# Waits put at their use, loads in another order, and one-head attentions on products of their weights, in a twelve-stage Perceiver kernel

## The chip, the cores and the metric

The kernel is one program on one core of a Trainium2 chip. The metric is the device time of one execution in microseconds (us). The core has five engines with a queue of instructions each: TensorE (PE), VectorE (DVE), ScalarE (ACT), GpSimd (POOL) and SyncE (SP). SP does nothing here but issue DMAs. The engines meet through semaphores; DMAs run on 16 DMA engines that all queues share.

## The reference

A residual stream `x` of 32 x 32 tokens by 256 features goes through four layers, each a cross-attention to a context of 32 batches x 257 rows x 192 features, a self-attention (or a scan) and a feed-forward part, all in float32, each on the layer norm of `x`:

```python
x = x + _L0_xattn_ref(_layernorm(x), ctx_768, ...)   # 16 heads
x = x + _L0_attn_ref(...)
x = x + _L0_ffn_ref(...)                             # fp4 weights and activations
x = x + _L1_xattn_ref(..., ctx_768, ...)             # 16 heads, clipped
x = x + _L1_attn_ref(...)                            # one head
x = x + _L1_ffn_ref(...)
x = x + _L2_xattn_ref(..., ctx_768, ...)             # 16 heads of 64
x = x + _L2_attn_ref(...)                            # a scan
x = x + _L2_ffn_ref(...)                             # experts with capacity
x = x + _L3_xattn_ref(..., ctx_768, ...)             # one head
x = x + _L3_attn_ref(...)                            # one head, below
x = x + _L3_ffn_ref(...)                             # eight experts
```

The two one-head self-attentions, each over the 32 tokens of a batch:

```python
# L1: f = x Wq^T, g = x Wk^T, h = x Wv^T
scores = einsum('bsd,btd->bst', f, g); beta = softmax(scores, axis=1)
o = gamma[0] * einsum('bsc,bst->btc', h, beta) + x
# L3: q, k, v = x W^T + b
qk = einsum('bsd,btd->bst', q, k)
theta = 0.5 + 0.2 * sigmoid(qk) + 0.15 * tanh(qk) + 0.1 * relu(qk)
out = einsum('bst,btd->bsd', softmax(theta), v) @ Wo.T + bo
```

## The kernel before

The 1024 tokens are `TILES` = 8 tiles of 128, one token to a partition, and `x` stays in SBUF for the whole program; one tile holds 4 batches (`PER_TILE`) of 32 tokens (`SEQ`). `CD` = 2 is the number of 128-row pieces of the 256 features. There are twelve stages one after the other: xattn0, attn0, the fp4 stage, xattn1, attn1, lowrank, xattn2, scan, moecap, xattn3, attn3, moe. A stage is one block with a function for each engine, which writes out by hand the order of that engine's queue: nothing is scheduled by a planner, and an instruction that waits holds everything behind it in its queue. A stage ends in a barrier of all five engines, SP's queue included. Each stage begins with a layer norm (class `Norm`, L95): statistics on DVE, 1/deviation on POOL, then transposes on PE (L190) with some dummy matmuls (L50, `warm` and `keep_busy`) around them.

What the change touches:

- **xattn2** is `stage_wide_attention` with `first=False`. SP's queue (L467 to L545) loads the weights wq and wk, then for the first four batches the two prepared layouts of the context (`load_parts`, L476 and L477), then `last`, wv and wo (L503 to L507), and then the raw rows of the context (`raw_last` L539, `load_rows` L537), of which DVE computes statistics (L888) for a later stage. DVE has those statistics in its queue between the units of the attention. A unit is one of 256 steps (batch and group of heads): scores (PE L668 to L672), their maximum (DVE L860), exp (ACT L785), the scaling (L790), transposes (PE L679), and the product with the context.
- **xattn1** is `stage_clipped_attention`. Its ACT queue waits for all of wv's loads ahead of the first unit of its loop:

```python
            for t in range(ALL + UNITS):
                j, s = divmod(t, UNITS)
                if t == 0:
                    act.wait_ge(wv_loaded, 64)
```

  The bias bv that these loads bring is read in `values` (L1297) alone, which comes first in unit 22. Here POOL scales the probabilities (L1110), DVE clips (L1345) and takes maxima (L1347).
- **attn1 and attn3** are `stage_one_head` (L1703). PE makes q^T and k^T in 8 blocks of two matmuls 128x512 (L1783), and between them v in 8 blocks of two matmuls 128x256 (L1790); then 64 matmuls of 32x32 for the scores, on four column groups of the array (L1799), dummy matmuls while DVE and ACT do the softmax, and then the product with v (L1809). attn1 adds it to x with one DVE instruction per tile (L1891). attn3 (`soft_theta`) scales it (L1901), transposes it (L1816), multiplies by wo (L1825), and adds (L1905). SP in attn3 first loads the stage's own eight tensors and then the expert weights of moe, 16 loads of 1024 KB (`ew.sp`, L2884 and L2885). moe's own small tensors (L2464 to L2467) are loaded in the moe stage; its gate matmuls (L2481) and two POOL instructions (L2472, L2473) wait for them.
- **The fp4 stage**: ACT makes |x| in four pieces (`x_parts`) and then copies the first transposed tile (`turned_x(0)`).
- **xattn3** has a ring of three tiles for the context (`RING`), in two layouts: keys (`load_keys`, L3255 to L3257) and rows (`load_rows`, L3263 and L3264). SP's queue issues both in turn. Keys of tile t may be overwritten when scores(t-3) are done, rows of tile t when the product pv(t-3) (L3363, L3366) is done:

```python
            load_rows(0)
            for t in range(1, TILES):
                load_keys(t)
                load_rows(t)
```

  Ahead of these it loads `last_stat` and `rstd` (L3267, L3269), which DVE and POOL wait for. The short weights of the stage (`ShortWeights`, L3159) are loaded in the scan stage, two stages earlier.

## Time and profile before

| what | value |
|---|---|
| median of 3 runs | 1784.45 us (1783.11 to 1786.04) |
| the profiled execution | 1781.79 us |
| its span in the trace | 1779.9 us, so 1.89 us lie around the span |
| busy shares | PE 89%, DVE 60%, ACT 48%, POOL 43% |
| mean granted clock of PE | 0.963 |
| xattn0, attn0, fp4 start at | 5.1, 351.2, 420.6 us |
| xattn1, attn1, lowrank start at | 519.3, 779.7, 818.9 us |
| xattn2, scan, moecap start at | 835.7, 1187.2, 1317.0 us |
| xattn3, attn3, moe start at | 1437.3, 1524.45, 1574.3 us |

A stage's start is its first layer-norm statistics instruction on DVE. All times in the rows are microseconds from the span's start. A timeline row joins neighbouring instructions of one form ("x8"); a matmul of these float32 tiles is two records, so "x8" is four matmuls. What stands in brackets at a row's end is how long the engine had been idle before it, and what released it. The granted clock is given as a share of the full 2.4 GHz: 1.00 is 2.4, 0.50 is 1.2 GHz.

### The profile page before, as it was taken

To read this page: it belongs to the slowest core of one execution; us is meant where nothing else is said; L and a number is where in the kernel's file an instruction comes from. 1 tells how busy PE (TensorE), PEld (TensorE's weight loads), DVE (VectorE), ACT (ScalarE), POOL (GpSimd) and SP (SyncE) were. 2 spreads that over 40 slices of the span, in tenths; PEclk is the share of its full clock that TensorE was granted. 3 is DMA by queue.
4 is the path that set the end of the run, shared out by engine and by line. 5 is a ranking of instruction groups with operands and counts; after the bars stand their busy time and mean duration, and the time that the engine had idled before them with its cause. 6 is when DMAs were issued, how large, how long until landed. Compare 5 with 4: busy or idle time off the path is not lost. (4 is left out here: it accounts for less than half of the span.)

```text
span 1779.9 us, 37424 instructions
## 1 busy us (share of the span) xinstructions
PE 1592.1 (89%) x13583; PEld 1347.5 (76%) x13583; DVE 1069.7 (60%) x3001; ACT 849.0 (48%) x2446; POOL 771.7 (43%) x924
## 2 busy tenths in 40 slices
PE   7999999888886999987799999989978968859998
PEld 6898998756556999955799988965658934549997
DVE  5888887446855888845676677647971132363332
ACT  5666666355335888842566666641003312213332
POOL 7656656243338999833211111116743411212332
PEclk9999999999998999999999999999988987989999
DMA  8555454110023334302433333325028265771222
GB/s 274 168 174 161 151 174 153 64 63 2 1 83 98 137 130 139 119 19 71 171 122 102 125 104 103 126 79 182 1 54 263 29 179 163 249 243 35 37 38 30
DMA packets 127221, 205.30 MB, mean 115 GB/s; under 512 B 21034, under 2 KB 92362, under 8 KB 126530
## 3 DMA queue, kind: packets, MB, share of 16 engines
q1 hardware_dynamic: 119746, 193.61, 33.4%
q0 software_dynamic: 6720, 8.79, 3.2%
q8 instruction: 111, 1.82, 0.4%
q14 instruction: 68, 0.56, 0.1%
q10 hardware_dynamic: 576, 0.52, 0.1%
HBM read 162.54 MB, written 41.14 MB: 114 GB/s over the span
## 5 line engine op out<-in xcount | busy, mean ns | idle before, releaser
L879 DVE TENSOR_SCALAR xattn_oT<-banks,xattn_last 128x256 f32<-128x256 f32 x256 | 111.7, 478 | 90.8 <-PE banks L699 90.6
L785 ACT ACTIVATE xattn_probs<-banks,xattn_negmax 128x257 f32<-128x257 f32 x256 | 123.6, 483 | 67.5 <-DVE xattn_negmax L860 67.5
L1110 POOL TENSOR_SCALAR xattn_probs<-xattn_probs,xattn_rsum 128x257 f32<-128x257 f32 x128 | 119.6, 935 | 30.0 <-DVE xattn_rsum L1351 29.8
L790 ACT ACTIVATE xattn_probs<-xattn_probs,xattn_rsum 128x257 f32<-128x257 f32 x256 | 131.8, 515 | 1.4 <-DVE xattn_rsum L864 1.4
L860 DVE TENSOR_REDUCE xattn_negmax<-banks 128x1 f32<-128x257 f32 x256 | 106.4, 415 | 34.7 <-PE banks L672 33.3
L679 PE MATMUL banks<-ident,xattn_probs 128*128 128x128 f32 x512 | 104.2, 286 | 8.5 <-ACT xattn_probs L790 8.0
L796 ACT CAST xattn_probsT_hi<-banks 128x256 fp32r<-128x256 f32 x256 | 95.4, 372 | 32.7 <-PE banks L679 28.6
L869 DVE TENSOR_TENSOR xattn_probsT_lo<-banks,xattn_probsT_hi 128x256 fp32r<-128x256 f32 x256 | 104.9, 410 | 9.8 <-ACT xattn_probsT_hi L796 8.7
L617 POOL COPY ctx_stat<-xattn_mv 128x2 f32<-128x2 f32 x32 | 6.0, 187 | 238.2 <-DVE xattn_mv L893 238.2
L668 PE MATMUL banks<-xattn_ctxT,xattn_qk_hi 128*128 128x258 f32 x256 | 93.9, 367 | 0.5 <-POOL xattn_ctxN L585 0.3
L573 POOL TENSOR_SCALAR xattn_ctxT<-xattn_rawT 128x514 fp32r<-128x514 f32 x32 | 49.8, 1558 | 98.7 <-issue 94.4
L694 PE MATMUL banks<-xattn_probsT_hi,xattn_ctxN 128*128 128x256 f32 x256 | 84.9, 332 | 5.0 <-DVE xattn_oT L879 3.4
L2288 POOL TENSOR_TENSOR scan_product<-scan_state,scan_qT 128x512 f32<-128x512 f32 x64 | 75.6, 1183 | 28.6 <-DVE scan_state L2430 28.2
L3022 PE MATMUL banks<-moe_xinT,moe_w_now 128*128 128x128 f32 x736 | 86.9, 277 | 0.0
L3022 PEld LDWEIGHTS banks<-moe_xinT,moe_w_now 128*128 128x128 f32 x736 | 85.1, 194 | 0.1
L650 PE MATMUL banks<-xattn_qT,xattn_wk 64*128 64x128 f32 x1024 | 73.3, 284 | 12.9 <-DVE xattn_qT L845 10.0
L2980 POOL DMA_INDIRECT out_dram<-moe_y_slots,moe_row_u x23 | 36.4, 1585 | 108.7 <-DVE moe_y_slots L3147 105.8
L3032 PE MATMUL banks<-moe_w,moe_hT 128*128 x368 | 83.1, 379 | 0.0
L2430 DVE TENSOR_TENSOR_SCAN scan_state<-banks,scan_decay 128x264 f32<-128x264 f32 x128 | 81.3, 688 | 1.7 <-PE banks L2316 0.4
L210 ACT COPY xnT<-banks 128x512 f32<-128x512 f32 x40 | 21.1, 585 | 121.9 <-PE banks L190 121.8
L650 PEld LDWEIGHTS banks<-xattn_qT,xattn_wk 64*128 64x128 f32 x1024 | 62.2, 187 | 22.0 <-issue 12.4
L715 PE MATMUL banks<-xattn_oT,xattn_wv 128*64 128x128 f32 x1024 | 69.4, 278 | 10.1 <-issue 7.5
(500 smaller groups left out, 5250.8 us busy)
## 6 DMA issues: line engine op xcount, KB each, us to landing
xattn_ctxT<-ctx_partsT SPq DMA_DIRECT2D x64, 516.0 KB, 4.0
xattn_ctxN<-ctx_partsN SPq DMA_DIRECT2D x64, 384.0 KB, 4.1
ctx_partsT<-xattn_ctxT SPq DMA_DIRECT2D x32, 516.0 KB, 2.8
moe_w<-in_L_ffn_W SPq DMA_DIRECT2D x16, 1024.0 KB, 13.6
ctx_partsN<-xattn_ctxN SPq DMA_DIRECT2D x32, 384.0 KB, 3.8
moecap_w_early<-in_L_ffn_w SPq DMA_DIRECT2D x10, 1024.0 KB, 9.2
xattn_N<-in_ctx_tiles SPq DMA_DIRECT2D x8, 776.0 KB
xattn_rawN<-in_ctx SPq DMA_DIRECT2D x32, 192.0 KB, 2.8
```

Source lines behind the costliest of these rows:

```text
L650: mm = nc.tensor.matmul(bank[:, k * P:(k + 1) * P], wk_s[r, h // 2, g % 2 * P:(g % 2 + 1) * P], qT[r, h // 2, :], start=True, stop=True, t ...
L668: nc.tensor.matmul(out, unit(qk1[0]), part(0, 0), start=True, stop=False)
L679: mm = nc.tensor.transpose(TB[n % 2][:, c * P:(c + 1) * P], probs[:, n % RING, c * P:(c + 1) * P], core.ident[:, :])
L694: nc.tensor.matmul(OB[:, 0:2 * P], first_hi(c), hi[:, c], start=(c == 0), stop=False)
L785: nc.scalar.activation(probs[:, n % RING, :], SB[n % 2][:, 0:KV], ACT.Exp, bias=negmax[:, n % RING:n % RING + 1], accum_out=psum[:, n % RI ...
L790: nc.scalar.mul(probs[:, n % RING, :], probs[:, n % RING, :], rsum[:, n % RING:n % RING + 1]).then_inc(norm_ready, 1)
L796: nc.scalar.copy(probsT[0][:, n // 2 % PAIRS, :, n % 2, :], TB[n % 2][:, 0:2 * P].rearrange("p (c n) -> p c n", c=2)).then_inc(probsT_hi_r ...
L860: nc.vector.tensor_reduce(negmax[:, n % RING:n % RING + 1], SB[n % 2][:, 0:KV], AX.X, ALU.max, negate=True).then_inc(negmax_ready, 1)
L869: nc.vector.tensor_tensor(lo, TB[n % 2][:, 0:2 * P].rearrange("p (c n) -> p c n", c=2), hi, ALU.subtract).then_inc(probsT_ready, 1)
L879: nc.vector.tensor_scalar(oT[k][:, heads, b, :], by_head(OB[:, k * 2 * P:(k + 1) * 2 * P]), last[:, k, j * PER_TILE + b:j * PER_TILE + b + ...
L1110: nc.gpsimd.tensor_scalar(probs[:, n % RING, :], probs[:, n % RING, :], rsum[:, n % RING:n % RING + 1], None, ALU.mult).then_inc(norm_read ...
L3022: mm = nc.tensor.matmul(H[n % 2][k][:, f * P:(f + 1) * P], w1_now[:, c, at:at + P], xinT[:, n % 2, c, :], start=(c == 0), stop=(c == CD - 1))
```

## The change

Five edits in five places, in program order:

1. **The fp4 stage**: on ACT `turned_x(0)` goes ahead of `x_parts(2)` and `x_parts(3)`.
2. **xattn1**: the wait on `wv_loaded` goes from the loop's start into `values`.
3. **attn1 and attn3**: instead of q and k the kernel forms the product of the two weights, Wq^T Wk (256 x 256, `product`, four matmuls 128x256, ahead of the transposes and behind a wait for all loads of the stage), and then t^T = (Wq^T Wk)^T x^T in 4 blocks of two matmuls 128x512 in place of 8; the scores are t^T against x^T. v is computed after the scores, while the softmax runs, and the dummy matmuls go. In attn3 Wo^T is multiplied into Wv as well, so that the transposes of the output, the matmuls with wo and their DVE and ACT instructions go, and one DVE instruction per tile is left; the biases are folded by 10 matmuls of one column and 2 of 256 (`fold_biases`), two POOL copies and five DVE instructions, and the scores of attn3 take two more matmuls per batch (`query_b`), 128 in place of 64.
4. **xattn2**: `raw_last` and the raw rows of batches 0 and 1 are loaded right behind the parts of batches 0 and 1; those of batches 2 and 3 stay last.
5. **xattn3**: `rstd` and `last_stat` are loaded with the short weights, in the scan stage, and DVE's waits for them go (POOL waits for the short weights in their place); the rows of tile t+3 are issued by ACT's queue, behind `normalise(t)`, and SP's queue has the keys alone from tile 4 on.

```diff
-            for k in range(1, CHUNKS):
+            x_parts(1)
+            turned_x(0)
+            for k in range(2, CHUNKS):
                 x_parts(k)
-            turned_x(0)
@@ xattn1, ACT @@
             def values(j, m):
                 act.wait_ge(m2_filled, j * 3 + m + 1)
+                act.wait_ge(wv_loaded, 64)
                 nc.scalar.activation(aT[:, m, :], M2[:, 0:P], ACT.Identity, bias=bv_s[:, m:m + 1]).then_inc(aT_ready, 1)
...
                 j, s = divmod(t, UNITS)
-                if t == 0:
-                    act.wait_ge(wv_loaded, 64)
                 if 0 <= t - EXP < ALL:
@@ stage_one_head, SP @@
+            for to, m in [(wq_s, wq), (wk_s, wk)]:
+                sp.dma_start(to[:, :, :], m.rearrange("(c p) n -> p c n", p=P)).then_inc(loaded, 16)
+            if soft_theta:
+                for n in range(3):
+                    sp.dma_start(b_s[:, n * CD:(n + 1) * CD], b_qkv[n]).then_inc(loaded, 16)
+            sp.dma_start(wv_s[:, :, :], wv.rearrange("(c p) n -> p c n", p=P)).then_inc(loaded, 16)
             if soft_theta:
                 sp.dma_start(wo_s[:, :, :], wo.rearrange("(c p) n -> p c n", p=P)).then_inc(loaded, 16)
                 sp.dma_start(bo_s[:, :], bo.partition_broadcast(P)).then_inc(loaded, 16)
@@ POOL @@
+            if soft_theta:
+                pool.wait_ge(loaded, 16 * LOADS)
+                for to, at in ((bq_wide, 0), (bv_wide, 2 * CD)):
+                    nc.gpsimd.tensor_copy(to[:, :, :], b_s[:, at:at + CD].unsqueeze(2).broadcast_to([P, CD, P])).then_inc(wide_ready, 1)
...
-                pool.wait_ge(loaded, 16 * LOADS)
+                pool.wait_ge(out_b_ready, 1)
@@ PE @@
+            def product(out, left, right):
+                for c in range(CD):
+                    for k in range(CD):
+                        mm = nc.tensor.matmul(out[:, c * D:(c + 1) * D], left[:, k, c * P:(c + 1) * P], right[:, k, :],
+                                              start=(k == 0), stop=(k == CD - 1))
+                return mm
+            def fold_biases():
...
+                for c in range(CD):
+                    for k in range(CD):
+                        nc.tensor.matmul(FOLD[:, c:c + 1], wk_s[:, k, c * P:(c + 1) * P], b_s[:, k:k + 1], start=(k == 0), stop=(k == CD - 1))
...
+                for k in range(CD):
+                    mm = nc.tensor.matmul(OUT, bv_wide[:, k, :], wo_s[:, k, :], start=(k == 0), stop=(k == CD - 1))
+                mm.then_inc(folded, 1)
...
             ln.warm(pe, 7)
+            pe.wait_ge(loaded, 16 * LOADS)
+            product(QK, wq_s, wk_s).then_inc(qk_done, 1)
             ln.pe(pe)
-            pe.wait_ge(loaded, 16 * LOADS)
+            if soft_theta:
+                fold_biases()
+                product(VO, wv_s, wo_s).then_inc(vo_done, 1)
+            pe.wait_ge(qk_ready, 1)
             for n in range(2):
                 pe.wait_ge(ln.xnT_ready, CD * (n + 1))
-                for f in range(4):
-                    k = 4 * n + f
-                    if k >= 2:
-                        pe.wait_ge(qk_ready, k - 1)
+                for f in range(CD):
                     for c in range(CD):
-                        mm = nc.tensor.matmul(bank[4 + k % 2], w[:, c, f * P:(f + 1) * P], core.xnT[:, c, n * HALF:(n + 1) * HALF],
...
+                for b in range(PER_TILE):
+                    own = slice(t * P + b * SEQ, t * P + (b + 1) * SEQ)
+                    parts = [(tT[:, c, own], core.xnT[:, c, own]) for c in range(CD)]
...
+                        parts += [(core.xnT[:, c, own], query_b[:, c, :]) for c in range(CD)]
+                    for k, (left, right) in enumerate(parts):
+                        mm = nc.tensor.matmul(S[b * SEQ:(b + 1) * SEQ, t * SEQ:(t + 1) * SEQ], left, right, start=(k == 0),
...
+                pe.wait_ge(vo_ready, 1)
+            for t in range(TILES):
+                if t >= 2:
+                    pe.wait_ge(v_ready, t - 1)
                 for c in range(CD):
-                    for b in range(PER_TILE):
...
-            mm.then_inc(scores_done, 1)
-            core.keep_busy(38 if soft_theta else 20, 5)
+                    mm = nc.tensor.matmul(bank[4 + t % 2][:, 0:D], core.xnT[:, c, t * P:(t + 1) * P], vo[:, c, :], start=(c == 0),
+                                          stop=(c == CD - 1))
+                mm.then_inc(v_done, 1)
...
+            for t in range(TILES):
+                pe.wait_ge(v_ready, t + 1)
+                if t >= 2:
+                    pe.wait_ge(x_done, t - 1)
+                nc.tensor.matmul(bank[t % 2][:, 0:D], probsT[:, t, :], v[:, t, :], start=True, stop=True).then_inc(pv_done, 1)
@@ ACT @@
-            ln.act(act)
...
+            ln.act(act, 0)
+            act.wait_ge(qk_done, 1)
+            nc.scalar.copy(qk[:, :, :].rearrange("p c n -> p (c n)"), QK).then_inc(qk_ready, 1)
+            ln.act(act, 1)
+            if soft_theta:
+                act.wait_ge(vo_done, 1)
+                nc.scalar.copy(vo[:, :, :].rearrange("p c n -> p (c n)"), VO).then_inc(vo_ready, 1)
+                act.wait_ge(fold_ready, 4)
+                act.wait_ge(relu_ready, 1)
...
+                if t == FIRST:
+                    act.wait_ge(sub_ready, 1)
+                    nc.scalar.activation(probs[:, :, :], sub[:, :, :], ACT.Exp).then_inc(probs_ready, 1)
+                values(t)
@@ DVE @@
+            if soft_theta:
+                dve.wait_ge(folded, 1)
+                nc.vector.tensor_copy(key_b[:, :], FOLD[:, 0:CD]).then_inc(fold_ready, 1)
+                nc.vector.tensor_copy(query_b[:, :, :], FOLD[:, CD:2 * CD].unsqueeze(2).broadcast_to([P, CD, SEQ])).then_inc(fold_ready, 1)
+                nc.vector.tensor_copy(both_b[:, :], FOLD[:, 2 * CD:2 * CD + 1]).then_inc(fold_ready, 1)
+                nc.vector.tensor_scalar(half_b[:, :], FOLD[:, 2 * CD:2 * CD + 1], 0.5, None, ALU.mult).then_inc(fold_ready, 1)
+                nc.vector.tensor_tensor(out_b[:, :], bo_s[:, :], OUT, ALU.add).then_inc(out_b_ready, 1)
+                dve.wait_ge(fold_ready, 4)
...
+            for t in range(TILES):
+                dve.wait_ge(pv_done, t + 1)
+                nc.vector.scalar_tensor_tensor(core.x[:, t, :], bank[t % 2][:, 0:D], factor[:, t:t + 1], rest[:, t, :],
@@ stage_wide_attention, SP @@
                     load_parts(n)
+                    if n == 0:
+                        sp.dma_start(raw_last[:, :], d["ctx_768"][:, KV - 1, :]).then_inc(raw_last_loaded, 16)
+                    if n < EARLY_ROWS:
+                        load_rows(n)
...
-                sp.dma_start(raw_last[:, :], d["ctx_768"][:, KV - 1, :]).then_inc(raw_last_loaded, 16)
-                for n in range(PER_TILE):
+                for n in range(EARLY_ROWS, PER_TILE):
                     load_rows(n)
@@ ShortWeights, SP @@
+        sp.dma_start(self.last_stat[:, :, :], self.cn.ends.rearrange("(p b) k -> p b k", p=1)).then_inc(self.loaded, 16)
+        for b in range(PER_TILE):
+            sp.dma_start(self.rstd[b * SEQ:(b + 1) * SEQ, :, :],
+                         self.cn.rows[2, b:BATCH:PER_TILE, 0:self.cn.KV].partition_broadcast(SEQ)).then_inc(self.loaded, 16)
@@ xattn3, SP, POOL, ACT, DVE @@
-            load_rows(0)
-            for t in range(1, TILES):
+            for t in range(RING):
+                load_rows(sp, t)
+                load_keys(t + 1)
+            for t in range(RING + 1, TILES):
                 load_keys(t)
-                load_rows(t)
...
-            pool.wait_ge(last_loaded, 16)
+            xw.ready(pool)
             for t in range(RING):
                 moments(t)
-            xw.ready(pool)
...
                     normalise(s - 2)
+                    if s - 2 + RING < TILES:
+                        load_rows(act, s - 2 + RING)
...
-            dve.wait_ge(rstd_loaded, 64)
-            dve.wait_ge(last_loaded, 16)
```

How the queues move at three places. In **xattn2**, SP's queue before, from the parts of the fourth batch on (`xattn_ctxT`, `xattn_ctxN` are the two layouts, `xattn_raw` the rows for the statistics):

```order
L476 DMA xattn_ctxT<-ctx_partsT 128x1032
L477 DMA xattn_ctxN<-ctx_partsN 128x768
L503 DMA xattn_last<-in_ctx_last 128x64
L504 DMA xattn_wv<-in_L_xattn_w_v 128x1024
L506 DMA xattn_wv<-in_L_xattn_w_v 64x1024 x2
L507 DMA xattn_wo<-in_L_xattn_w_o 128x8x256
L539 DMA xattn_raw_last<-in_ctx 32x192
L537 DMA xattn_raw<-in_ctx 128x2x192 x4
```

and with the change, from the parts of the first batch on:

```order
L477 DMA xattn_ctxT<-ctx_partsT 128x1032
L478 DMA xattn_ctxN<-ctx_partsN 128x768
L508 DMA xattn_raw_last<-in_ctx 32x192
L484 DMA xattn_raw<-in_ctx 128x2x192
L477 DMA xattn_ctxT<-ctx_partsT 128x1032
L478 DMA xattn_ctxN<-ctx_partsN 128x768
L484 DMA xattn_raw<-in_ctx 128x2x192
```

`raw_last` and the rows of batch 0 stood behind the parts of all four batches and the five loads of last, wv and wo; now only the parts of batch 0 stand ahead of them, and the rows of batch 1 follow the parts of batch 1.

In **xattn3**, SP's queue before, where the keys of tile 3 come (first three rows), its rows, and the keys of tile 4:

```order
L3255 DMA xattn_T<-in_ctxT_tiles 128x1028
L3256 DMA xattn_T<-in_ctxT_tiles 64x1028
L3257 DMA xattn_T<-ctx_rows 2x1028
L3263 DMA xattn_N<-in_ctx_tiles 128x1552
L3264 DMA xattn_N<-in_ctx_ends 1x776
L3255 DMA xattn_T<-in_ctxT_tiles 128x1028
L3256 DMA xattn_T<-in_ctxT_tiles 64x1028
L3257 DMA xattn_T<-ctx_rows 2x1028
```

and with the change the keys of tiles 3 and 4 in a row, with nothing of `xattn_N` between them:

```order
L3296 DMA xattn_T<-in_ctxT_tiles 128x1028
L3297 DMA xattn_T<-in_ctxT_tiles 64x1028
L3298 DMA xattn_T<-ctx_rows 2x1028
L3296 DMA xattn_T<-in_ctxT_tiles 128x1028
L3297 DMA xattn_T<-in_ctxT_tiles 64x1028
L3298 DMA xattn_T<-ctx_rows 2x1028
```

The rows of tile 3 now stand in ACT's queue, behind the scaling of tile 0's product (L3482):

```order
L3476 ACTIVATE xattn_probs<-xattn_scaled,xattn_negmax 128x257
L3482 ACTIVATE xattn_o_norm<-banks,xattn_shift,xattn_rsum 128x192
L3287 DMA xattn_N<-in_ctx_tiles 128x1552
L3288 DMA xattn_N<-in_ctx_ends 1x776
L3476 ACTIVATE xattn_probs<-xattn_scaled,xattn_negmax 128x257
```

In **attn1**, PE's queue before, from the dummy matmuls of the layer norm on (`attn_w` holds wq, wk and wv); the pair of rows L1783 and L1790 comes eight times in all:

```order
L50 MATMUL banks<-ident 128x256 x16
L190 MATMUL banks<-ident,xn 128x128 x16
L1783 MATMUL banks<-xnT,attn_w 128x512 x2
L1790 MATMUL banks<-attn_w,xnT 128x256 x2
L1783 MATMUL banks<-xnT,attn_w 128x512 x2
L1790 MATMUL banks<-attn_w,xnT 128x256 x2
```

and from the last of them to the end of the stage:

```order
L1790 MATMUL banks<-attn_w,xnT 128x256 x2
L1799 MATMUL banks<-attn_kT,attn_qT 32x32 x64
L50 MATMUL banks<-ident 128x256 x20
L1809 MATMUL banks<-attn_v,attn_probsT 128x256 x8
```

With the change the whole stage is (`attn_qk` is the product of the weights, `attn_tT` is t^T; L1846 makes v):

```order
L50 MATMUL banks<-ident 128x256 x16
L1791 MATMUL banks<-attn_wk,attn_wq 128x256 x4
L190 MATMUL banks<-ident,xn 128x128 x16
L1823 MATMUL banks<-xnT,attn_qk 128x512 x8
L1837 MATMUL banks<-xnT,attn_tT 32x32 x64
L1846 MATMUL banks<-attn_wv,xnT 128x256 x16
L1854 MATMUL banks<-attn_v,attn_probsT 128x256 x8
```

Eight of the sixteen matmuls 128x512 are gone, four of 128x256 have come ahead of the transposes, and v's sixteen stand behind the scores, where the 20 dummy matmuls stood.

## Rows read from the trace of the kernel before

**Rows 1.** page, part 2: busy tenths of the DMA engines in 40 slices of 44.5 us
```profile
DMA  8555454110023334302433333325028265771222
```

**Rows 2.** timeline, ACT in xattn1; start us, us, engine line op out<-in xcount [idle before <-releaser]
```profile
540.98 0.48 ACT L1270 ACTIVATE xattn_kT<-banks,xattn_bk 128x258 fp32r<-128x258 f32 x1 [10.89 <-DMA xattn_bv<-in_L_xattn_bv_cols]
```

**Rows 3.** timeline, PE in xattn1
```profile
542.03 0.58 PE L1158 MATMUL banks<-xattn_ctxT,xattn_wk_hi 128*128 128x258 f32 x1 [8.12 <-DVE xattn_kT L1338]
```

**Rows 4.** timeline, POOL in xattn1
```profile
542.94 0.94 POOL L1110 TENSOR_SCALAR xattn_probs<-xattn_probs,xattn_rsum 128x257 f32<-128x257 f32 x1 [8.36 <-DVE xattn_rsum L1351]
```

**Rows 5.** timeline, PE in attn1
```profile
781.43 1.37 PE L50 MATMUL banks<-ident 128*128 128x256 bf16 x8 [0.20 <-DVE attn_ln_stats L142]
...
785.33 1.19 PE L190 MATMUL banks<-ident,xn 128*128 128x128 f32 x8 [1.03 <-DVE xn L155]
786.64 1.96 PE L1783 MATMUL banks<-xnT,attn_w 128*128 128x512 f32 x4
...
806.50 1.03 PE L1790 MATMUL banks<-attn_w,xnT 128*128 128x256 f32 x4
808.08 1.29 PE L1799 MATMUL banks<-attn_kT,attn_qT 128*32 128x32 f32 x128 [0.55 <-ACT attn_v L1833]
...
812.61 0.70 PE L1809 MATMUL banks<-attn_v,attn_probsT 128*128 128x256 f32 x2 [0.95 <-DVE attn_probsT L1882]
```

**Rows 6.** timeline, DVE at the end of attn1
```profile
817.37 0.92 DVE L1891 SCALAR_TENSOR_TENSOR x<-banks,attn_rgamma,attn_x_plus 128x256 f32<-128x256 f32 x2 [0.36 <-PE banks L1809]
```

**Rows 7.** timeline, SP's queue in attn1: its last load
```profile
780.78 0.47 SPq L1757 DMA_DIRECT2D attn_gamma<-in_L_attn_gamma  x1
```

**Rows 8.** DMA issues from 779 to 790, the last load: KB, median us to landing
```profile
attn_gamma<-in_L_attn_gamma SPq DMA_DIRECT2D x1, 0.5 KB, 3.8
```

**Rows 9.** timeline, DVE in xattn2
```profile
863.08 0.36 DVE L888 BATCH_NORM_STATS2 xattn_stats<-xattn_raw 128x6 f32<-128x192 f32 x1 [6.74 <-DMA xattn_raw<-in_ctx]
```

**Rows 10.** timeline, SP's queue in xattn2
```profile
846.55 7.29 SPq L539 DMA_DIRECT2D xattn_raw_last<-in_ctx  x1
```

**Rows 11.** timeline, PE in xattn2
```profile
864.82 0.48 PE L679 MATMUL banks<-ident,xattn_probs 128*128 128x128 f32 x1 [5.34 <-ACT xattn_probs L790]
```

**Rows 12.** timeline, PE in xattn3
```profile
1461.21 0.64 PE L3339 MATMUL banks<-xattn_T,xattn_qk 66*32 66x257 f32 x8
...
1477.87 1.11 PE L3338 MATMUL banks<-xattn_T,xattn_qk 128*32 128x257 f32 x8 [6.32 <-DMA xattn_T<-ctx_rows]
...
1500.12 0.67 PE L3338 MATMUL banks<-xattn_T,xattn_qk 128*32 128x257 f32 x8 [0.71 <-DMA xattn_T<-ctx_rows]
1500.56 0.67 PE L3339 MATMUL banks<-xattn_T,xattn_qk 66*32 66x257 f32 x8
```

**Rows 13.** timeline, SP's queue in xattn3
```profile
1457.26 0.35 SPq L3255 DMA_DIRECT2D xattn_T<-in_ctxT_tiles  x1
...
1468.63 0.36 SPq L3263 DMA_DIRECT2D xattn_N<-in_ctx_tiles  x1
...
1469.36 0.36 SPq L3255 DMA_DIRECT2D xattn_T<-in_ctxT_tiles  x1
```

**Rows 14.** stretches: us, length, busy of PE PEld DVE ACT POOL, clock, DMA share, GB/s
```profile
1477.80:1497.00 19.20, 19.14 (x123) 9.13 (x124) 4.75 (x16) 5.31 (x13) 3.38 (x8) 0.51 0.54 176
1531.70:1574.30 42.60, 39.42 (x294) 27.21 (x294) 17.93 (x36) 10.10 (x29) 5.22 (x8) 1.00 1.05 375
420.60:466.00 45.40, 35.46 (x186) 25.46 (x187) 42.81 (x84) 20.98 (x44) 17.26 (x16) 0.92 0.00 1
```

**Rows 15.** timeline, POOL in attn3 and at moe's start
```profile
1531.41 5.51 POOL L1767 TENSOR_TENSOR x<-x,attn_bo 128x256 f32<-128x256 f32 x8 [1.17 <-DMA attn_b<-in_L_attn_bv_cols]
...
1579.38 0.44 POOL L2472 CAST moe_gate_up_to_b<-moe_gate_up_to 128x256 bf16<-128x256 f32 x1 [0.27 <-DMA moe_gate_up_to<-in_up_to]
```

**Rows 16.** timeline, SP's queue at the end of attn3
```profile
1565.23 2.35 SPq L2885 DMA_DIRECT2D moe_w<-in_L_ffn_W  x1
```

**Rows 17.** timeline, PE at moe's start
```profile
1580.94 3.64 PE L2481 MATMUL banks<-moe_gate_w,xnT 128*128 128x8 f32 x32
```

195 lines of the change are left out of this document (76 added, 119 removed).

## The prediction

> **What bounds the kernel now.** TensorE is busy for 89% of the span, and the stages run one after the other behind barriers, so a stage's time changes only where its own last chain of waits changes. I read the timelines of the stages that the change touches, engine by engine, and looked for the longest idle time in each and what ended it. Then I read the granted clock of the stretch behind it.
>
> In xattn1 ACT stood for 10.89 us until the last load of wv had landed [rows 2], though it had only to copy keys. PE then lacked them for 8.12 us, and POOL stood for 8.36 us [rows 3, 4]. In attn1 PE is hardly idle; its own work is the time [rows 5]. In xattn2 DVE stood for 6.74 us at a statistics instruction whose rows of the context had not landed [rows 9], with the maxima of the attention behind it, and PE stood for 5.34 us [rows 11]. The DMA in question lay behind `raw_last`, which SP took 7.29 us to issue because the queue was full [rows 10]. In xattn3 PE stood for 6.32 us for the keys of tile 4 [rows 12]. SP issued them only at 1469.36, since ahead of them in its queue the rows of tile 3 waited until 1468.63 for a product [rows 13]. The keys' own condition (scores of tile 1) was met at 1461.9 [rows 12]. After that idle time PE worked at half clock for 19.2 us without a gap [rows 14]. In attn3 PE's work is again the time, but the DMA engines are full throughout with moe's weights [rows 14].
>
> **The change part by part.** The sum is made against the profiled execution, 1781.79 us, 2.66 under the median of 1784.45; I carry the difference over.
>
> *xattn1, the wait.* ACT has nothing to wait for but its maxima, so the first units start as soon as PE and POOL ran dry, 8.12 or 8.36 us earlier. wv is needed from unit 22 on, and a unit costs POOL 0.94 us at least [rows 4], so the moved wait ends over 20 us after the load has landed; nobody queues behind it. Next in the ramp is POOL, before as after. I take **8.3**. The low end is one POOL step less, 7.4; the high end 9.4, if the half clock behind the idle time was worth 1 us.
>
> *attn1, the product.* PE's dummies end at 782.8 [rows 5]; the last load is issued at 780.78 and lands 3.8 us later, at 784.6 [rows 7, 8]. Eight blocks took from 786.64 to 807.5 [rows 5], 2.61 us each: by columns 1.74 for two matmuls 128x512 and 0.87 for two of 128x256. So the product (four of 256) ends at 786.35, the transposes (1.2 us per half) and the copies of their results let t^T start at 789.0, four blocks of 1.74 end at 796.0, the scores (1.29) [rows 5] with the last DVE copy at 797.4, and v (8 x 0.87) at 804.3. The softmax took 3.2 us from the scores' end to the first product with v (809.4 to 812.6), so it hides under v, where dummies filled the time before. From that product to the end it was 5.68 us (812.61 to 818.29) [rows 5, 6]: the end is at 809.8 to 810.0 against 818.29, **8.5** saved. The 1.8 us that PE now waits for the loads are in that. Unknown is the scores' order, in which two matmuls in a row now go to the same column group. If those don't overlap at all, the four-fold overlap of 1.29 us is lost and it is 5.2: a gain of 4.6. In xattn3 the scores come in just this order, two in a row to one group, and 8 matmuls of 257 columns (two rows x8) took 1.11 us, 1500.12 to 1501.23 [rows 12], a third of what single ones would take by the block's price (8 x 0.44), so I count nothing. The high end is 9.4, with part of the load wait hidden. These 128 records in 1.29 us are 10 ns each. The Trainium skill, "TensorE: Matmul & The Clock Gate", section "Wait — 56ns, not 53.3ns?", says that matmuls never start less than about 25 ns apart; by it the scores would cost 3.2 us and attn1 gain 6.6. The trace disagrees for four column groups, and it decides.
>
> *xattn2, the order.* The first rows now follow 2.2 MB of weights and bias and 0.9 MB of parts, 9 us at 375 GB/s from the stage's start, and land before 848, while DVE reaches them at 856.3 [rows 9]. PE's 5.34 us go, and part of the half clock behind them. I take **6.4**, with 5.3 (the idle time alone) and 8.0 (6.74 and all of the clock) as ends. The other parts come 0.2 to 0.6 MB later, at 375 GB/s [rows 14] up to 1.6 us, before anything asks for them; batch 2's rows are asked for only units later.
>
> *xattn3, the queues.* The keys of tile 4 are issued at 1461.9 instead of 1469.36. They took 8.5 us to land, so they are there at 1470.4, before PE comes to them at 1471.55. The gap of 6.32 goes, the later 0.71 as well [rows 12], and with no gap the 19.14 us of PE work run at the clock of 1.00 instead of 0.51 [rows 14]: 9.4 us. Together 16.4; I take **15.4**, because at full speed the chain through ACT and DVE between two tiles ends last now and then (the tile that begins at 1500.12 is such a one). The low end is 11.7, the gaps and half the clock. ACT issues ten DMAs more, 0.36 us each on SP's queue [rows 13], and is busy for 5.31 of 19.2 us [rows 14]. It adds no wait, since `normalise(t)` has waited for the same product. The rstd loads (1.03 MB) go to the scan, where the DMA engines are a fifth to half busy (slices 26 to 29) [rows 1]: nothing; without that cover 2.8 us.
>
> *attn3, the products.* The eight loads have landed at 1531.4 [rows 15]. From there, with the prices of attn1: two products 3.5, transposes 2.2, folded biases 0.9 plus twenty records of one column (between 10 ns each, as the scores, and 114 ns, as the gate's 32 records in 3.64 us [rows 17]: 0.2 to 2.3, I take 1.5, nearer the row of like shape), t^T 7.0, scores 2.6, v 7.0, output 5.7. The end is at 1561.8, 12.5 us earlier. But SP's queue, which takes part in the barrier, gets rid of its last weight load at 1567.6 [rows 16], and the 16.8 MB at 375 GB/s [rows 14] flow until about 1576.5. moe's own four small loads stand behind them, so I expect them at about 1578.3; POOL had them at 1579.4 [rows 15]. The gate matmuls started at 1580.94 [rows 17]: 2.4 us can be saved. PE is idle for some 6 us twice on the way, as long as in xattn3 [rows 12], which can put these matmuls on half clock, up to 3.6 more. I take **1.0**, between a loss of 1.2 and a gain of 6.6 (small loads that don't queue, with the barrier at 1567.6).
>
> *fp4.* **0**: DVE is busy for 42.8 of 45.4 us there [rows 14] and hides a tile turned earlier. Ends: 2.6 gained, 0.5 lost (one ACT instruction of that size) [rows 2].
>
> Sum: 8.3 + 8.5 + 6.4 + 15.4 + 1.0 = 39.6; the profile would show 1742.2, the median be **1744.9**. All low ends give 27.8, all high ones 49.8: 1756.7 and 1734.7.
>
> **The rivals.** (A) *moe's small loads don't queue behind the weights*: the barrier's 6.6 us come through, 1739.3. For it: issued behind the barrier at 1574.3, they had landed by 1579.1 [rows 15], 4.8 us for four of them, not far from an unloaded one's 3.8 [rows 8]; against it, by then the weights were nearly through. (B) *xattn3's transfers stay late*: rows of tile 3 and keys of tile 4 now flow at once. The Trainium skill, "DMA: Bandwidth & Descriptors", section "Issuing engines are not separate DMA queues", says that another issuing engine saves only sequencer time; the trace agrees as far as SP's issues are short. But what is saved is a wait of SP, not its issuing. It decides if the 2.3 MB of keys 3, rows 3 and keys 4 need more than the 14.3 us from 1457.26 to 1471.55, that is under 165 GB/s, and 176 were moved on demand alone and 375 under load [rows 14]. Then some 4 us of the 15.4 are left: 1756.3. (C) *Same-group matmuls don't overlap*: 3.9 lost in attn1, 1748.8. (D) *Another wait takes the place* in xattn1 and xattn2 (the change doesn't do there what it says): 14.7 less, 1759.6; the bracketed releasers speak against it. (E) *Slower*: PE enters xattn3 at half clock, behind the idle time at the start of the stage, and without the former gaps stays there. About 44 us of its 87 are full-clock work; at half clock they double, and the 9.4 aren't won: 39.6 - 9.4 - 44 = -13.8, so 1798.2. It decides from 30 us of such work on. Before, 19.2 us of it passed so, with a busy PE throughout [rows 14], and by 1500.12 it was back to full.
>
> **How the numbers follow.** My case 72%, A 10%, B 10%, C 4%, D 2%, E 2%. The range is 1735 to 1757, the ends of the bounds, which take in A, B and C; outside lie D, E and the case that several terms miss the same way. A measurement of this kernel tells 0.2% (3.6 us) from no change; only E is slower, and only a sum of misses in all five terms is as small as that: faster 0.97, same 0.015, slower 0.015.
>
> **What would show it.** Right: ACT's L1270 in xattn1 without a wait for the load of bv; attn1 some 30 us long from its first statistics; no statistics instruction of xattn2 released by a DMA in its first units; scores(4) of xattn3 right behind their forerunners with the granted clock at 1.00 up to the stage's end; moe's gate matmuls 2 to 3 us earlier relative to attn3's start, SP's last weight load still the end of attn3. Wrong: a DMA as releaser of PE in xattn3, a stretch at 0.50 of over 5 us there, or attn3 ending before SP's queue is free.

## The result

Over four runs each, the changed kernel took 1755.58 us in the median (1754.59 to 1757.62), the kernel before 1783.78 us (1779.44 to 1786.04): a ratio of 0.9843, 95% interval 0.9814 to 0.9872. So 28.2 us were gained where 39.6 were forecast. The profiled execution took 1754.59 us, its span 1752.7, so again 1.89 us lie around it, and 27.2 us are gone from the span.

The start of attn1 in the kernel before is 779.4 in the trace; the 779.7 in the table of stages above is a slip.

| stage, us from its first statistics to the next stage's | before | after | difference | forecast |
|---|---|---|---|---|
| attn0 (untouched) | 69.4 | 67.8 | -1.6 | 0 |
| fp4 | 98.7 | 97.3 | -1.4 | 0 |
| xattn1 | 260.1 | 253.4 | -6.7 | -8.3 |
| attn1 | 39.5 | 30.8 | -8.7 | -8.5 |
| lowrank (untouched) | 16.8 | 18.1 | +1.3 | 0 |
| xattn2 | 351.5 | 344.7 | -6.8 | -6.4 |
| moecap (untouched) | 120.3 | 118.9 | -1.4 | 0 |
| xattn3 | 87.1 | 86.1 | -1.0 | -15.4 |
| attn3 | 49.9 | 49.5 | -0.4 | -1.0 for both |
| moe | 205.6 | 205.4 | -0.2 | |

xattn0 and scan moved by 0.3 us or less. Three terms came nearly as forecast, one, the largest, hardly at all.

**xattn1.** ACT's queue in the profile after (start, length, engine, line, operation, tiles; in brackets the idle time before and its releaser):

```profile
526.67 0.48 ACT L1274 ACTIVATE xattn_kT<-banks,xattn_bk 128x258 fp32r<-128x258 f32 x1 [0.52 <-PE banks L1166]
529.39 0.48 ACT L1274 ACTIVATE xattn_kT<-banks,xattn_bk 128x258 fp32r<-128x258 f32 x1 [2.25 <-PE banks L1166]
529.77 0.50 ACT L1280 ACTIVATE xattn_probs<-xattn_clamped,xattn_negmax 128x257 f32<-128x257 f32 x1
```

The second key copy no longer waits for the load of bv [rows 2], and the first exp starts at 529.77. PE's queue at its one long wait, and two stretches around it (stretch, length, busy PE, PEld, DVE, ACT, POOL, clock, DMA share, GB/s):

```profile
539.92 0.69 PE L1190 MATMUL banks<-ident,xattn_probs 128*128 128x128 f32 x2 [3.70 <-POOL xattn_probs L1114]
```

```profile
516.20:540.00 23.80, 15.75 (x112) 11.73 (x113) 16.03 (x52) 11.47 (x31) 17.64 (x26) 0.96 0.81 240
540.00:543.00 3.00, 2.33 (x10) 2.03 (x10) 1.04 (x4) 0.64 (x3) 3.00 (x5) 0.50 0.00 0
```

The 8.12 us [rows 3] are gone. What PE waits for in the ramp is POOL, as before: four waits of 6.7 us in all (0.73, 1.37, 3.70, 0.93), where there had been three of 4.6 (0.36, 3.29, 0.92). Here its clock still falls to 0.50.

**attn1.** PE's queue after:

```profile
774.22 1.99 PE L1791 MATMUL banks<-attn_wk,attn_wq 128*128 128x256 f32 x8 [0.57 <-DMA attn_gamma<-in_L_attn_gamma]
```

```profile
785.80 1.71 PE L1837 MATMUL banks<-xnT,attn_tT 128*32 128x32 f32 x128
787.44 7.17 PE L1846 MATMUL banks<-attn_wv,xnT 128*128 128x256 f32 x32
794.46 1.03 PE L1854 MATMUL banks<-attn_v,attn_probsT 128*128 128x256 f32 x4
```

The product starts at 774.22, 4.6 us after the stage's first statistics; the last load kept PE waiting for 0.57 us behind its dummies. The scores took 1.71 us instead of 1.29 [rows 5], v 7.0 us, and the tail is 6.0 us from the first product with v to the stage's end, where it was 6.3 [rows 5, 6].

**xattn2.** DVE and PE at the place of [rows 9] and [rows 11]:

```profile
839.28 0.36 DVE L892 BATCH_NORM_STATS2 xattn_stats<-xattn_raw 128x6 f32<-128x192 f32 x1
```

```profile
842.43 0.44 PE L683 MATMUL banks<-ident,xattn_probs 128*128 128x128 f32 x2
```

No idle time stands at either; the first statistics instruction follows the first maximum at once. SP issued the small load `raw_last` in 0.47 us at its new place, where it had taken 7.29 us behind all the weights [rows 10]; the rows left at the end still held SP for 7.66 us, with no wait of DVE or PE for them in the first 40 us of the stage.

**xattn3.** PE's queue from the scores of tile 4 on (L3368 was L3338, L3404 was L3374):

```profile
1446.75 0.66 PE L3368 MATMUL banks<-xattn_T,xattn_qk 128*32 128x257 f32 x8
...
1460.57 0.67 PE L3368 MATMUL banks<-xattn_T,xattn_qk 128*32 128x257 f32 x8 [0.77 <-DMA xattn_T<-ctx_rows]
...
1463.60 0.47 PE L3404 MATMUL banks<-ident,xattn_o_norm 128*128 128x128 f32 x1 [1.45 <-ACT xattn_o_norm L3482]
...
1478.59 0.33 PE L3404 MATMUL banks<-ident,xattn_o_norm 128*128 128x128 f32 x1 [1.03 <-ACT xattn_o_norm L3482]
```

The 6.32 us of [rows 12] are gone: the scores of tile 4 start 35.0 us into the stage instead of 40.5, and those of tile 7 at 48.9 instead of 62.8. So 13.9 us had been won at 1460.57. From there to the stage's end it then took 37.3 us, where before it had taken 24.3 from 1500.12. DVE and POOL at that place:

```profile
1462.04 0.69 DVE L3566 TENSOR_TENSOR x<-x,banks 128x512 f32<-128x512 f32 x1 [4.43 <-POOL x L3324]
...
1462.84 0.16 DVE L3561 SCALAR_TENSOR_TENSOR xattn_shift<-banks,xattn_rsum 128x1 f32<-128x1 f32 x1
```

```profile
1460.31 0.20 POOL L3315 COPY xattn_N<-ctx_stat 128x16 f32<-128x16 f32 x1 [3.51 <-DMA xattn_N<-in_ctx_ends]
...
1460.60 1.41 POOL L3324 TENSOR_TENSOR x<-x,xattn_bo 128x256 f32<-128x256 f32 x2
```

DVE's addition to x (L3566) had stood for 4.43 us, waiting for POOL's bias additions (L3324), which DVE wants all eight of before the first. POOL's queue has them in pairs, and between the pairs it waits for rows: the last pair stands behind the rows of tile 5, which landed at 1460.3. Behind DVE's wait stood the shift of tile 4, and behind that ACT's scaling and PE's transposes of the same tile. In the kernel before the same two instructions had been 8.5 us apart, the last pair ending at 1489.7 and DVE's first addition starting at 1498.26:

```profile
1488.34 1.39 POOL L3294 TENSOR_TENSOR x<-x,xattn_bo 128x256 f32<-128x256 f32 x2
```

```profile
1498.26 0.69 DVE L3534 TENSOR_TENSOR x<-x,banks 128x512 f32<-128x512 f32 x1 [1.83 <-PE banks L3395]
```

With the change DVE reached that addition at 1457.6, 45.9 us into the stage instead of 59.1, while POOL's last pair ended at 50.3 us instead of 52.4. Then came the clock:

```profile
1446.00:1460.50 14.50, 13.80 (x171) 7.35 (x159) 5.43 (x20) 7.05 (x17) 3.60 (x10) 1.00 1.01 325
1463.60:1476.60 13.00, 12.80 (x59) 6.72 (x63) 2.25 (x8) 3.44 (x8) 0.33 (x2) 0.50 0.19 63
1476.60:1480.00 3.40, 2.37 (x26) 1.03 (x18) 0.43 (x3) 1.31 (x3) 0.00 (x0) 1.00 0.00 0
1480.00:1489.50 9.50, 8.47 (x39) 4.94 (x39) 0.33 (x2) 2.15 (x5) 0.00 (x0) 0.50 0.00 0
```

In these stretches the clock was at half for 22.5 us in place of the 19.2 of [rows 14], behind idle times of PE of 0.77 and 1.45 us, and of 1.03 us. The first line shows why the rows of tile 5 were late: the DMA engines were busy for the whole 14.5 us.

**attn3 and moe.** PE's queue at three places, and SP's last weight load:

```profile
1506.55 3.78 PE L1791 MATMUL banks<-attn_wk,attn_wq 128*128 128x256 f32 x8 [5.29 <-DMA attn_bo<-in_L_attn_bo]
```

```profile
1530.53 0.19 PE L1837 MATMUL banks<-attn_query_b,xnT 128*32 128x32 f32 x1 [3.39 <-issue]
```

```profile
1554.32 1.92 PE L2510 MATMUL banks<-moe_gate_w,xnT 128*128 128x8 f32 x16 [0.32 <-DMA moe_gate_up_to<-in_up_to]
```

```profile
1541.33 1.05 SPq L2914 DMA_DIRECT2D moe_w<-in_L_ffn_W  x1
```

The eight loads had landed 8.7 us after the stage's start, not 7.0 as before (1531.4 against 1524.45). Why they came later no run here tells. The first product then took 3.78 us instead of 1.9. In the middle of the scores PE stood for 3.39 us with no releaser that the profile knows ("issue"), and the 256 records of the scores took 9.7 us in all, not 2.6. The stage's compute ended at 1547, so it ended the stage, 4.6 us behind SP's queue; the gate's matmuls waited 0.32 us for moe's small load. They started 56.5 us after attn3's start, as in the kernel before.

### The profile page after: what moved, and what is told of

Same layout as the page of the kernel before. It is cut to its first block and busy times, and to the rows that moved or that the text cites. A ratio compares the mean times of both kernels' runs of the same rounds, so it can differ in the third digit from the quotient of the medians.

```text
span 1752.7 us, 37478 instructions
## 1 busy us (share of the span) xinstructions
PE 1579.5 (90%) x13621; PEld 1342.1 (77%) x13621; DVE 1061.8 (61%) x2990; ACT 846.3 (48%) x2433; POOL 773.6 (44%) x926
## 3 DMA queue, kind: packets, MB, share of 16 engines
q1 hardware_dynamic: 119016, 189.62, 33.3%
## 5 line engine op out<-in xcount | busy, mean ns | idle before, releaser
L577 POOL TENSOR_SCALAR xattn_ctxT<-xattn_rawT 128x514 fp32r<-128x514 f32 x32 | 49.9, 1560 | 98.1 <-issue 92.9
L2317 POOL TENSOR_TENSOR scan_product<-scan_state,scan_qT 128x512 f32<-128x512 f32 x64 | 75.7, 1183 | 27.8 <-DVE scan_state L2459 27.3
L719 PE MATMUL banks<-xattn_oT,xattn_wv 128*64 128x128 f32 x1024 | 69.4, 278 | 10.2 <-issue 7.6
```

## The experiments

Twelve kernels ran, four to a chip, each beside runs of the kernel before on the same chip. Ratios are to that kernel, with their 95% intervals. A stage is read as in the table above. No kernel leaves a part of the computation out.

### The changed kernel and the kernel before, once more

> The changed kernel itself once more, beside the three that follow, so that they can be compared on one chip, and to see how far the stages of one and the same program move. The first comparison gave a ratio to the kernel before of 0.9843 (0.9814 to 0.9872): 0.984 again, and stage lengths within 2 us of the first profile's in each stage, attn3 excepted, where kernels with the same code showed 49.5 to 53.0 us.

1757.94 us, ratio 0.9857 (0.9834 to 0.9880). xattn1 251.7, attn1 33.1, xattn2 344.6, xattn3 78.0, attn3 48.7, moe 207.5, and the untouched attn0 at 72.4 against 67.8: the total repeats, but four stages beside attn3 moved by more than the 2 us expected: xattn3 by 8.1, attn0 by 4.6, attn1 by 2.3 and moe by 2.1, in the same program.

> The kernel before itself, for a second profile of its stages beside the three that follow. One and the same code moved in the seven profiles of the changed stages by 1.5 us in xattn1, 2.5 in attn1, 3.0 in xattn2, 9.0 in xattn3 (77.1 to 86.1) and 4 in attn3. Expected within such distances of the first profile: xattn1 260, attn1 39.5, xattn2 351.5, xattn3 80 to 90, attn3 with moe 255.5.

One run, 1792.49 us. xattn1 260.7, attn1 39.5, xattn2 351.1, attn3 and moe 255.5 repeat the first profile. xattn3 was 97.0 us instead of 87.1, outside the 80 to 90 expected. PE's two long waits for keys in it:

```profile
1477.51 1.11 PE L3338 MATMUL banks<-xattn_T,xattn_qk 128*32 128x257 f32 x8 [5.46 <-DMA xattn_T<-ctx_rows]
...
1498.36 1.11 PE L3338 MATMUL banks<-xattn_T,xattn_qk 128*32 128x257 f32 x8 [2.97 <-DMA xattn_T<-ctx_rows]
```

So a stage is judged by all profiles of its code, not by one. Here they are for the two stages in question, every kernel of the study sorted by the code that it has there:

| code of xattn3 | us in each profile | mean | us at half clock from 38 us on |
|---|---|---|---|
| before (before, before_again, undo5) | 87.1, 97.0, 84.8 | 89.6 | 20.5, 41.0, 13.7 |
| the bias first alone (bias_first_no5) | 91.9 | | 27.3 |
| edit 5 (after, after_again, undo124, scores_outer, wait_two, hold_weights, old_attn3) | 86.1, 78.0, 83.9, 84.6, 77.1, 80.6, 79.7 | 81.4 | 27.3, 10.2, 23.9, 27.3, 13.7, 17.1, 13.7 |
| edit 5 and the bias first (bias_first, joined, joined_old3) | 74.2, 73.8, 72.3 | 73.4 | 3.4, 3.4, 0 |

The last column adds up what the granted clock in each trace shows behind the 38th us of the stage. Within one code the long profiles are those with more half clock. DVE's first addition waited for POOL's last pair for 4.3 to 5.6 us in all seven profiles of edit 5, and not at all in the other seven.

| code of attn3 | attn3 and moe together, us | mean |
|---|---|---|
| before (before, before_again, old_attn3, joined_old3) | 255.5, 255.5, 259.4, 261.5 | 258.0 |
| edit 3 (after, after_again, undo5, bias_first, undo124, bias_first_no5) | 254.9, 256.2, 258.9, 259.4, 257.4, 257.4 | 257.4 |

### Edit 5 taken back

```diff
-                    if s - 2 + RING < TILES:
-                        load_rows(act, s - 2 + RING)
+            for t in range(1, TILES):      # SP: keys and rows in turn, rstd ahead of them
+                load_keys(t)
+                load_rows(t)
```

> The changed kernel with edit 5 (xattn3) taken back, everything else kept. In the profile after, xattn3 is 86.1 us from its first statistics to attn3's, against 87.1 before. Theory (edit 5 gave its whole time back through a new wait and a later fall of PE's clock): xattn3 is about 87 us here and the run 1 us slower than the changed kernel, about 1756.6. Rival (the other edits brought xattn3 into a worse state of the clock, and edit 5 is worth its 15 us): xattn3 is near 100 us and the run about 1770.

1764.89 us, ratio 0.9891 (0.9845 to 0.9936); xattn3 84.8. The stage came as in the theory, the time halfway to the rival's. By this one profile edit 5 is worth nothing. By the table above it is worth 8.2 us, and the whole kernel agrees with the table: 0.9891 against 0.9843 and 0.9857 with it is some 0.4%, 7 us, though the intervals meet. Three profiles of a code that spread over 12 us don't give this size to better than some microseconds.

### POOL's bias additions first in xattn3

```diff
             for t in range(TILES):
                 nc.gpsimd.tensor_tensor(core.x[:, t, :], ..., bo[:, :], ALU.add).then_inc(bo_added, 1)
-                if t % 2 and t // 2 + RING < TILES:
-                    moments(t // 2 + RING)
-            for t in range(RING + TILES // 2, TILES):
+            for t in range(RING, TILES):
                 moments(t)
```

> The changed kernel, but in xattn3 POOL adds the bias to all eight tiles of x before it waits for the rows of tiles 3 to 7. In the profile after, DVE stood 4.43 us until 1462.04 for that addition, with the shift of tile 5 behind it, and PE's clock fell to 0.50 for 13.0 and 9.5 us from 1463.6 on. Theory A (that wait is what broke the chain, and without it PE stays at full clock): the tail from scores of tile 7 to the end of the stage takes 24 us as before the change instead of 37, xattn3 73 to 75 us, the run about 1743. Theory B (the clock falls anyway, since PE waits shortly and often there): only 1.5 to 3 us are gained, xattn3 about 84, the run about 1753.5. Theory C (POOL's wait hides behind the transfers): nothing, 1755.6.

1750.79 us, ratio 0.9791 (0.9746 to 0.9836); xattn3 74.2 us, the number of theory A for the stage. The run is not at A's 1743: attn3 (53.0) and xattn2 (347.6) were 3.5 and 2.9 us longer than in the first profile of the changed kernel, whose code they share. POOL's additions, PE's queue behind the scores of tile 7, and the clock from there on:

```profile
1435.55 5.51 POOL L3324 TENSOR_TENSOR x<-x,xattn_bo 128x256 f32<-128x256 f32 x8
```

```profile
1463.57 1.08 PE L3366 MATMUL banks<-xattn_T,xattn_qk 128*32 128x257 f32 x8 [1.50 <-DMA xattn_T<-ctx_rows]
...
1466.13 0.42 PE L3402 MATMUL banks<-ident,xattn_o_norm 128*128 128x128 f32 x1
...
1471.59 0.33 PE L3402 MATMUL banks<-ident,xattn_o_norm 128*128 128x128 f32 x1 [0.55 <-ACT xattn_o_norm L3480]
...
1476.04 0.33 PE L3402 MATMUL banks<-ident,xattn_o_norm 128*128 128x128 f32 x1 [1.03 <-ACT xattn_o_norm L3480]
```

```profile
1463.50:1471.00 7.50, 7.43 (x56) 3.93 (x56) 1.73 (x6) 2.04 (x5) 0.97 (x6) 0.77 0.35 116
1471.00:1489.00 18.00, 13.95 (x95) 8.43 (x94) 3.12 (x9) 5.62 (x13) 0.00 (x0) 1.00 0.00 0
```

The eight additions are one row at 1435.55. The transposes of tile 4 (L3402, 1466.13) follow the others without a wait where PE had stood for 1.45 us. The short waits of 0.55 and 1.03 us are still there, and a longer one for the keys of tile 7 (1.50 us), with half clock for a few us; from 1471.0 on the clock is 1.00 to the end of the stage. In joined_old3, below, with the same code of xattn3, it is 1.00 for the whole of that part:

```profile
1448.00:1486.90 38.90, 33.46 (x317) 18.85 (x309) 11.37 (x38) 15.14 (x36) 1.63 (x10) 1.00 0.43 142
```

Theory C falls (the wait did cost) and B too.

### The same without edit 5

> The kernel bias_first (POOL's bias additions of xattn3 ahead of its waits for rows) with edit 5 taken back: xattn3 is that of before but for the place of the additions. Theory (edit 5 takes the wait for the keys of tile 4, 6.3 us with half clock behind it, and only the two together give the gain): xattn3 stays at 84 to 87 us, and PE waits over 5 us for xattn_T. Rival (the additions alone are worth it, edit 5 nothing): xattn3 74 to 76.

1766.32 us, ratio 0.9887 (0.9855 to 0.9919), xattn3 91.9 us. PE's queue and two stretches:

```profile
1454.73 1.11 PE L3365 MATMUL banks<-xattn_T,xattn_qk 128*32 128x257 f32 x8 [5.42 <-DMA xattn_T<-ctx_rows]
```

```profile
1476.02 1.11 PE L3365 MATMUL banks<-xattn_T,xattn_qk 128*32 128x257 f32 x8 [3.43 <-DMA xattn_T<-ctx_rows]
```

```profile
1454.70:1462.00 7.30, 7.27 (x61) 2.98 (x61) 1.70 (x6) 1.72 (x4) 0.33 (x2) 0.50 0.47 139
...
1475.00:1486.00 11.00, 9.98 (x54) 4.64 (x55) 1.50 (x5) 2.04 (x5) 0.33 (x2) 0.50 0.14 53
```

The waits for keys are those of the kernel before, with half clock behind each. The stage is longer than the 84 to 87 expected, but neither it (91.9 lies among the 84.8 to 97.0 of the kernel before) nor the kernel (0.9887, with undo5 at 0.9891) shows a gain by the bias first alone. With edit 5 the two are worth 16.2 us by the stages (89.6 to 73.4). The whole kernels agree, and here the intervals lie apart: 0.9887 against 0.9791 in bias_first is 17 us for edit 5 once the additions stand first. That is the forecast's mechanism and, with the second half that the change lacked, its size.

### Edits 1, 2 and 4 taken back

> The changed kernel with edits 1, 2 and 4 (fp4, xattn1, xattn2) taken back; its stages are read one by one. After against before: fp4 97.3 and 98.7 us, xattn1 253.4 and 260.1, xattn2 346.1 and 351.5. Theory (edits 2 and 4 are worth 6.7 and 5.4, fp4 is chance): xattn1 260, xattn2 351.5, fp4 anywhere from 97.3 to 98.7 as attn0, which nobody touched, had 69.4 and 67.8; the run about 1768. Rival (edit 1 is worth 1.35): fp4 98.7, the run 1769.

1771.78 us, ratio 0.9910 (0.9876 to 0.9945): xattn1 258.8, xattn2 351.7, fp4 99.0. (The 346.1 for xattn2 with the change, in what was expected, is a slip: the trace has 344.7.) The ratio lies 0.5 to 0.7% above the changed kernel's, 9 to 12 us, which agrees with the two stages together. All profiles with edit 2 have xattn1 at 251.5 to 253.4, those without at 258.8 to 260.7: 7.6 us between the means (252.3 of eleven, 259.9 of three). With edit 4 xattn2 is 344.6 to 347.6, without it 351.1 to 351.7: 6.0 us. fp4 was 97.3 to 100.7 with edit 1 and 98.7 to 100.7 without: nothing that these can tell, and attn0, which no kernel changes, moved between 67.5 and 72.4.

### The scores round the column groups

```diff
-                for b in range(PER_TILE):
-                    for k, (left, right) in enumerate(parts):
+                for k in range(last):          # 2 pieces in attn1, 4 in attn3
+                    for b in range(PER_TILE):
```

> The changed kernel, but the scores of the one-head attentions go round the four column groups again (piece outer, batch inner), with the same matmuls. In the profile after they took 1.64 us for 128 records in attn1 (1.29 before) and 9.6 us for 256 records in attn3, 3.4 of them one idle time with no releaser shown. Theory (two or four in a row to one group overlap less): 1.3 us in attn1, and in attn3 2.6 us plus the idle time of 3.4, so 6; the run 0.3 + 3.6 = 4 us faster if nothing else gates attn3, about 1751.6. Rival (the order is free, and it is the mere number of instructions that is late to come in while the DMA engines are full): attn1 1.6, attn3 9.6, 1755.6.

1760.49 us, ratio 0.9858 (0.9817 to 0.9898): the 4 us forecast for the run are not there. attn1's scores took 1.62 us instead of 1.71; attn3's 8.05 instead of 9.7:

```profile
1531.85 0.34 PE L1836 MATMUL banks<-attn_query_b,xnT 128*32 128x32 f32 x9 [4.95 <-issue]
```

The idle time is 4.95 us now, so without it the 256 records took 3.1 us in this order and 6.3 in the other. In attn3, where four matmuls in a row go to one group, that order costs 3.2 us; in attn1, with two in a row, 0.1. The theory's 1.3 in attn1 and the rival's free order are both wrong; the rival's other half, instructions that come late, is taken up under the weights held back, below. Of the 3.2 PE gave 1.6 back as a longer idle time, and moe gave back the rest, at the gate's matmuls:

```profile
1556.03 6.60 PE L2509 MATMUL banks<-moe_gate_w,xnT 128*128 128x8 f32 x32 [1.68 <-DMA moe_gate_up_to<-in_up_to]
```

They had waited 1.68 us for moe's small load and then took 6.6 us, at a clock of 0.53, where they took 3.7 in the first profile at 1.00; attn3 is 46.9 us and moe 209.8, together 256.7.

### Moe's weights held back until the scores are done

```diff
+                sp.wait_ge(scores_done, 1)
                 ew.sp(sp)
```

> The changed kernel, but SP waits in attn3 until the scores are done before it issues moe's 16 weight loads, so that the DMA engines are idle while PE works through the scores; moe then waits for its weights, and the run as a whole is slower by 10 to 25 us, which is not what is asked. Asked is the one idle time of 3.2 to 5.0 us with no releaser (issue) among the 256 records of the scores, which was there in all five profiles of this code and in none of the 128 records of attn1. Theory (PE ran out of instructions, whose own transfers had to pass DMA engines that were full): no such idle time, the scores 4 to 6 us instead of 8.0 to 9.6, and as the loads land sooner, no half clock at the product. Rival (the idle time belongs to the instructions themselves): it stays at 3 to 5 us.

One run, 1781.18 us, the weights being late as foreseen. In the scores:

```profile
1524.27 0.19 PE L1838 MATMUL banks<-attn_query_b,xnT 128*32 128x32 f32 x1 [0.38 <-issue]
```

```profile
1520.70:1526.50 5.80, 5.42 (x258) 5.27 (x257) 0.75 (x1) 0.00 (x0) 0.00 (x0) 1.00 0.02 6
```

```profile
1524.00:1533.70 9.70, 6.31 (x258) 6.16 (x257) 0.75 (x1) 0.00 (x0) 0.00 (x0) 0.87 1.06 373
```

An idle time of 0.38 us is left of 3.0 to 3.7 in this order, and the scores took 5.8 us. The DMA share around them is 0.02 instead of 1.06.

The profile lists the fetching of instructions as DMA queues of their own. Queue q8 moves one packet of 16384 bytes for about every 254 records of PE (112 packets in the changed kernel), so it carries PE's instructions. In scores_outer PE stood from 1526.90 to 1531.85. The DMA queues from 1526.9 to 1529.2, and from 1529.2 to 1530.4 (packets, MB, share of 16 engines):

```profile
q1 hardware_dynamic: 563, 0.87, 105.1%
...
q1 hardware_dynamic: 400, 0.41, 102.9%
q8 instruction: 1, 0.02, 6.0%
```

For 2.3 us only moe's weights (q1) moved; then came one packet of instructions, from 1529.21 to 1530.37, and PE went on 1.5 us later. It is so in every kernel with these scores. PE stopped behind the same record, the 151st of 256. With full DMA engines the packet started 3.7 to 4.3 us behind the first score, in nine profiles, with idle ones 1.2 us, and PE went on 1.2 to 1.5 us behind the packet's end in all ten. So PE stood because its next instructions came late through full DMA engines, and a faster order of the scores only made it wait longer. The Trainium skill, "Runtime: NRT & Kernel Launch", "Instruction fetch mechanics", says that each engine's sequencer fetches its instructions in blocks of 16 KiB over a DMA queue of its own, and that crossing a block's end is mostly hidden. The packets agree with such blocks; that it is hidden holds here at a DMA share of 0.02 (0.38 us), not at 1.06 (3.39 us). The half clock at the first product did not go (3.69 us for it): the loads, issued later than foreseen (SP took 2.26 us over one of them), landed as late as ever, 9.1 us into the stage.

### PE's first wait for two loads alone

```diff
-            pe.wait_ge(loaded, 16 * LOADS)
+            pe.wait_ge(two_loaded, 32)         # Wq and Wk
             product(QK, wq_s, wk_s).then_inc(qk_done, 1)
             ln.pe(pe)
+            pe.wait_ge(loaded, 16 * LOADS)
```

> The changed kernel, but in the one-head stages PE waits only for Wq and Wk ahead of the first product, and for the rest behind the transposes. In the profiles of the changed code PE stood for 0.57 us in attn1 and for 4.2 to 6.3 us in attn3 until bo had landed, and in attn3 the product and part of what followed then ran at 0.50 of the clock (3.78 us where 1.9 are usual). Theory (the wait for all loads cost the wait and the clock, and compute is what ends attn3): attn3 5 to 8 us shorter, 43 to 46 us; attn1 0.5 to 1.5 shorter. Rival (SP's queue with moe's weights, free at 44.6 us from the stage's start, and moe's small loads behind them end it anyway): attn3 46 us, and moe longer by as much as attn3 goes below 48, so that the two together lose 3 us at most of 255 to 259.

1754.61 us, ratio 0.9845 (0.9822 to 0.9869), beside 0.9857 for the changed kernel on the same chip: no difference that these intervals show. In attn3:

```profile
1494.89 1.99 PE L1791 MATMUL banks<-attn_wk,attn_wq 128*128 128x256 f32 x8 [1.62 <-DMA attn_wk<-in_L_attn_Wk]
1496.72 1.91 PE L190 MATMUL banks<-ident,xn 128*128 128x128 f32 x16
1500.49 1.21 PE L1800 MATMUL banks<-attn_b,attn_wk 128*128 128x1 f32 x8 [1.86 <-POOL attn_bv_wide L1776]
```

The product starts after 1.62 us instead of 5.29 and takes 1.99 us at full clock. But the folding of the biases then waits for the rest of the loads, and it and what follows run at a clock near half (0.56 from 1500.5 to 1506). attn3 49.1, moe 209.2: the theory's 5 to 8 us aren't there, and attn3 isn't at the rival's 46 either.

### attn3 with the stage of before

> The changed kernel with the one-head stage of before in attn3 alone; attn1 keeps the product of the weights. Attn3 and moe together were 255.5 us before and 254.9, 256.2, 257.4, 258.9 and 259.4 in five profiles of the changed code. Theory (in attn3 the change brings nothing or costs: its wait for the loads with the clock behind it, and scores of 9.6 us in place of 1.3, eat what the matmuls save): attn3 49.9, attn3 with moe 255 to 256, the run equal to the changed kernel or up to 2 us faster. Rival (the product saves there as in attn1): the run 5 us slower.

1759.97 us, ratio 0.9860 (0.9833 to 0.9887), attn3 and moe 52.7 and 206.7, together 259.4. With the table above: 258.0 for the old form, 257.4 for the new. In attn3 edit 3 is worth nothing that these runs can tell, the interval being 5 us to either side; its whole gain is in attn1, 39.5 us in both profiles of before and 30.8 to 33.3 in the eight of the unmended new form.

### Joined

```diff
-        for e in range(self.E):                # in attn3
+        for e in range(self.E - 1):            # the last expert's two loads in moe,
+        ...                                    # behind the stores of x
```

> The changed kernel with what has come out so far put together: POOL's bias additions of xattn3 ahead of its waits for rows, the scores of the one-head stages round the column groups, PE's first wait for Wq and Wk alone, and the last expert's two weight loads (2 of 16) issued in moe, behind its small loads and the stores of x. xattn3 74 us instead of 84 to 86. attn3: loads 5 to 8 and scores 1.6 to 3 us less, and SP's queue free 5 us sooner, so 41 to 43 us. moe: if its small loads stood behind the weights until now, they land before PE has its transposes and the gate's matmuls start at about 6.7 us from the stage's start with no wait for a DMA, moe 204 to 206 us. The run 18 to 22 us faster than the changed kernel, a ratio of 0.973 to 0.975 to the kernel before. Rival (what is won ahead of the weights comes back as a wait for the last of them ahead of the dense part of moe): xattn3's 11 us only, 0.978.

1745.86 us, ratio 0.9790 (0.9768 to 0.9813), the fastest of all, 0.7% (12 us) below the changed kernel on the same chip, where 18 to 22 us were forecast. xattn3 73.8, attn3 45.6, moe 208.4:

```profile
1538.13 5.24 PE L2511 MATMUL banks<-moe_gate_w,xnT 128*128 128x8 f32 x32
```

The gate's matmuls start 6.5 us into moe with no wait, as foreseen. But so they did, at 6.6 to 6.7, in four kernels whose weights had not been moved and whose attn3 took 51 to 53 us. They take 5.24 us, and the first gathered tile comes 30.5 us into the stage (27.6 to 28.1 in those four and in the first profile). So it is near the rival's number, 0.978: xattn3's gain, with little more from attn3.

> The changed kernel with the bias additions first in xattn3, the one-head stage of before in attn3, and in attn1 PE's first wait for two loads and the scores round the column groups. If attn3's new form is worth nothing, this is as fast as the kernel joined (ratio 0.979, 0.9768 to 0.9813): xattn3 74, attn1 29.5, attn3 with moe 255.5, so 8 to 12 us faster than the changed kernel. If attn3's new form with its two mends is worth something (joined had 45.6 and 208.4, together 254.0), this is 1.5 us slower than joined.

1750.11 us, ratio 0.9798 (0.9779 to 0.9816): xattn3 72.3, attn1 30.7, attn3 and moe 261.5. The two intervals overlap almost wholly. On the stages alone the new form, with its mends and the late loads, is 7.5 us better here (254.0 against 261.5), on the ratio 0.08%, 1.4 us; the size stays open.

## Why the prediction was right in sign and range, and where it failed

The kernel became faster, as forecast, and 1755.58 lies in the range of 1735 to 1757, but near its end: 28.2 us were gained, and all low ends together were to give 27.8. (The sums of the ends left fp4's own ends out; with them they are 27.3 and 52.4.) It is in the range by some luck. The largest term came in below its own low end, and the others stayed above theirs. That rival B's 1756.3 stands for the gain measured, 28.2, is luck too: the keys of tile 4, by which B was to decide, were in time.

- **xattn1, forecast 8.3:** 6.7 in the first pair, 7.6 by the means. The mechanism was right; the term was sized by the idle times of PE and POOL, and in the ramp behind PE then waited 2.2 us more for POOL than before. It is about the low end of that term (7.4).
- **attn1, forecast 8.5:** 8.7 in the pair, 7.4 by the means of eight. Its end was foreseen some 31 us into the stage and came at 30.8 to 33.3. The scores cost 0.4 us more than the count; rival C, 3.9 us for groups that don't overlap, did not come: two in a row cost 0.1. The 25 ns from start to start that the Trainium skill states ("TensorE: Matmul & The Clock Gate", "Wait — 56ns, not 53.3ns?") were not seen here either: 13 ns a record.
- **xattn2, forecast 6.4:** 6.8 and 6.0. Right, with its cause.
- **xattn3, forecast 15.4:** 1.0 in the pair, 8.2 by the means. The step that failed is the sentence "with no gap the 19.14 us of PE work run at the clock of 1.00". The gap of 6.32 went as forecast, and 13.9 us had been won by the scores of tile 7. But a wait that no row of before showed came up, of 4.3 to 5.6 us on DVE in all seven profiles: POOL's last bias additions stood behind the rows of tile 5. DVE came to its first addition 13.2 us earlier in the stage, these additions only 2.1 us earlier. I had asked of the moved rows only whether ACT's queue suffers, not what on POOL stands behind their landing. And the clock was at half for 10.2 to 27.3 us in the second half of the stage, where I had it at full. With the additions first it was so for 3.4 us at most, and the forecast's 16.4 came out as 16.2. Which of the short waits tips the clock stays open.
- Rival B was half right. The transfers did not miss the keys of tile 4, but from tile 5 on DMA was at its limit (share 1.01, 325 GB/s): rows issued by ACT at 1450.3 landed at 1460.3. That agrees with the section of the Trainium skill that rival B drew on, "DMA: Bandwidth & Descriptors", "Issuing engines are not separate DMA queues": another engine saved SP's waiting, and the bytes took their time.
- **attn3, forecast 1.0:** 0.6 in the pair, 0.6 by the means. The number was right for a wrong reason. I had the compute end at 37 us, with SP's queue as the end at 43; the compute took 49. Three prices failed: all loads 8.7 us after the start instead of 7.0, half clock at the products behind a wait of 5.29 us (3.78 us for 1.7), and the scores, 9.7 us for 2.6, of which 3.2 us are the order of the groups and 3.4 an idle time while PE's instructions came late. SP's end was foreseen at 43.1 and came at 44.6. In scores_outer, where the compute came down to 46.9, the gate's matmuls waited 1.68 us for moe's small load, the next barrier that I had named.
- **fp4, forecast 0:** nothing that can be told from chance.

Of the signs that were to show it right, those of xattn1, attn1, xattn2 and of the scores of tile 4 came. The clock at 1.00 to the end of xattn3, the gate's matmuls 2 to 3 us earlier and SP's last load as the end of attn3 did not. Of the signs of being wrong two came: a DMA as releaser of PE in xattn3 (0.77 us, for the keys of tile 7) and a stretch at 0.50 of over 5 us there. The third, an attn3 that ends before SP's queue is free, did not: it ended 4.6 us behind it, by its own compute.

The runs lack 11.4 us of the forecast, the first pair of profiles 12.4. In that pair xattn3 lacks 14.4 and xattn1 1.6, and the stages forecast at nothing give some 3.5 back. By the means xattn3 lacks 7.2, attn1 1.1, xattn1 0.7, xattn2 and attn3 0.4 each, and the rest lies in the spread of single profiles. Where the forecast erred, it took the next wait for the one seen in the old trace.

## What to carry to other kernels

When transfers are moved, follow each landing to every engine that waits for it, also to a queue that does something unrelated behind that wait: here the bias of x, which needed no transfer, stood behind rows of the context. Put work that needs nothing ahead of waits, and test a gain from removed waits by the end of the stage, not by the wait's disappearance. Compare a stage over several profiles of the same code before an edit is called worthless or good: xattn3 spread over 9 us without a change. And where a stage spreads so, read its granted clock first: here the long profiles were those with more half clock.

## What the runs showed of the hardware that I had not expected

- PE's granted clock fell to 0.50 behind idle times of 0.77 and 1.45 us, and of 1.03 us (the changed kernel, from 1463.6 and 1480.0 on), and in bias_first it stayed at 1.00 with waits of 0.55 and 1.03 us. The Trainium skill, "TensorE: Matmul & The Clock Gate", Part 1, ties the half rate to an idle array, and the half clock behind PE's waits of 3.70 and 5.29 us agrees with it. Which short wait tips it these runs don't tell, and the same code gave xattn3 in 77.1 to 86.1 us.
- While moe's weight loads kept the DMA engines full, PE stood for 3.0 to 5.0 us once in the middle of 256 small matmul records, in all nine profiles that had them together, until a 16384-byte packet of its instructions had come; with the engines idle for 0.38 us.
- Matmuls of 32 columns on four column groups: 10.0 ns a record before, 12.7 ns in the new operands' round order, 13.4 with two in a row to one group, 24 ns with four in a row (6.3 us for 256; 21 ns, 5.4 us, with the DMA engines idle).
